# Where a pair's edge scores stand in the second layer of a two-layer graph network

## What is computed

```python
h = jnp.einsum('ni,hio->hno', x, W)                    # 4 heads of 64
attn_src = jnp.einsum('hno,hod->hn', h, a_src)
attn_dst = jnp.einsum('hno,hod->hn', h, a_dst)
e = attn_src[:, src_idx] + attn_dst[:, dst_idx]
e = jnp.where(e >= 0, e, NEG_SLOPE * e) * edge_weight[None, :]
e_exp = jnp.exp(e - jnp.max(e))
denom = jax.ops.segment_sum(e_exp.T, dst_idx, num_segments=num_nodes).T
alpha = e_exp / (denom[:, dst_idx] + 1e-10)
msg = h[:, src_idx] * alpha[..., None]                 # summed over dst, per head
```

## Time and profile before

| | us |
|---|---|
| median of 3 runs | 2435.32 |
| lowest, highest | 2430.52, 2443.21 |
| profiled execution | 2453.26 |
| its span | 2451.1 |
| mean granted TensorE clock | 0.886 |
| PE, DVE, POOL, ACT busy, share of the span | 79%, 62%, 60%, 56% |
| gathers of the second layer (L1351), 391 | 371.1 busy, 346.0 idle before |

### The profile page before, as it was taken

The page is one execution under the profiler, slowest core; times in us unless marked ns, Lnnn a source line. Parts: engine busy times, 40 slices in busy tenths (PEclk is TensorE's granted clock), DMA queues, the critical chain, the costliest instruction groups (busy, mean ns, idle before and its releaser), DMA issues. The chain is left out here.

```text
span 2451.1 us, 40398 instructions
## 1 busy us (share of the span) xinstructions
PE 1929.3 (79%) x12892; PEld 1704.4 (70%) x12892; DVE 1509.6 (62%) x3750; ACT 1382.8 (56%) x2780; POOL 1470.6 (60%) x1204
## 2 busy tenths in 40 slices
PE   7699999999999999999999999955134545544560
PEld 6588899988999999999999999954123333433440
DVE  6466666666666666666666666645155445444575
ACT  2488888888888888888888888845000000000012
POOL 0317778777777777767777777532645645654623
PEclk9899999999999999999999999977567667766785
DMA  5878877777777777777777777665434434444523
GB/s 198 287 204 182 196 165 169 170 166 166 160 160 158 159 159 159 157 161 154 158 159 158 158 158 159 131 158 138 107 87 120 129 106 123 129 110 109 134 83 108
DMA packets 236167, 370.81 MB, mean 151 GB/s; under 512 B 35853, under 2 KB 168935, under 8 KB 235949
## 3 DMA queue, kind: packets, MB, share of 16 engines
q0 software_dynamic: 101232, 188.20, 38.7%
q1 hardware_dynamic: 134717, 179.94, 24.4%
HBM read 270.57 MB, written 97.45 MB: 150 GB/s over the span
## 5 line engine op out<-in xcount | busy, mean ns | idle before, releaser
L1316 POOL DMA_INDIRECT accA<-ystage,to_a x391 | 650.2, 1663 | 231.0 <-issue 108.0
L1322 POOL DMA_INDIRECT GA<-TA,src_c x391 | 425.1, 1087 | 328.7 <-issue 93.3
L1351 POOL DMA_INDIRECT Hg<-HT,src_c x391 | 371.1, 949 | 346.0 <-DVE xb L913 168.7
L1861 ACT ACTIVATE drop<-neg_m 128x1 f32<-128x1 f32 x49 | 14.5, 295 | 627.3 <-DVE neg_m L908 517.1
L1420 PE MATMUL bank<-h1h,W1h 128*128 128x512 f32 x882 | 349.2, 396 | 1.3 <-DVE h1l L539 0.7
L1422 PE MATMUL bank<-h1h,W1l 128*128 128x512 f32 x882 | 348.0, 395 | 0.0
L1421 PE MATMUL bank<-h1l,W1h 128*128 128x512 f32 x882 | 347.0, 393 | 0.0
L539 DVE TENSOR_TENSOR h2l<-h2f,h2h 128x512 fp32r<-128x512 f32 (+1 forms) x294 | 202.8, 690 | 202.4 <-issue 87.3
L1628 PE MATMUL bank<-xb,in_window 128*128 128x260 f32 (+1 forms) x782 | 249.7, 475 | 70.3 <-issue 69.2
L539 DVE TENSOR_TENSOR h1l<-h1f,h1h 128x512 fp32r<-128x512 f32 x294 | 194.9, 690 | 131.2 <-ACT h1h L1698 112.9
L1628 PEld LDWEIGHTS bank<-xb,in_window 128*128 128x128 f32 (+1 forms) x782 | 182.4, 241 | 122.4 <-issue 87.3
(11 more groups left out here) (209 smaller groups left out, 5235.1 us busy)
## 6 DMA issues: line engine op xcount, KB each, us to landing
TW<-TB SPq DMA_DIRECT2D x196, 203.0 KB
ef<-in_eT SPq DMA_DIRECT2D x97, 256.0 KB
bcast_i<-in_src_row SPq DMA_DIRECT2D x97, 256.0 KB
HB<-hist SPq DMA_DIRECT2D x98, 130.0 KB
rel<-RL SPq DMA_DIRECT2D x97, 128.0 KB
rem<-RD SPq DMA_DIRECT2D x48, 256.0 KB
TB<-stB SPq DMA_DIRECT2D x24, 406.0 KB
accA<-zeros SPq DMA_DIRECT2D x4, 1677.0 KB, 13.0
```

The source lines that it names most:

```text
L1316: return pool.indirect_dma_start(out=table, out_offset=bass.IndirectOffsetOnAxis(ap=rows, axis=0), in_=sums, in_offset=None, compute_op=AL ...
L1322: pool.indirect_dma_start(out=GA[0:n, b % (GAR * BLOCKS_PER_GROUP), :].bitcast(f32), out_offset=None, in_=TA, in_offset=bass.IndirectOffse ...
L1351: pool.indirect_dma_start(out=Hg[0:n, slot, :], out_offset=None, in_=HT, in_offset=bass.IndirectOffsetOnAxis(ap=src_c[0:n, b:b + 1], axis= ...
```

## The change

On DVE `edge_scores(q+2)` moves from behind `carry_window(2q-1)` to between `running_maximum(q+1)` and `weighted_rows(2q+1)`, and `one_hot(q+3)` moves ahead of `window_rows(q+1)`. On PE `spread_maxima(q+2)` moves between the window sums of the pair's two groups. No function changes inside, no instruction, wait or buffer is added or taken away.

```diff
@@ vector
                 if 0 <= q + 1 < NQ:
                     running_maximum(q + 1)
+
+                if 0 <= q + 2 < NQ:
+                    edge_scores(q + 2)
                 if 0 <= q < NQ:
                     weighted_rows(2 * q + 1)
                 if 0 <= q - 1:
                     carry_window(2 * q - 1)
-                if 0 <= q + 2 < NQ:
-                    edge_scores(q + 2)
+                if q + 3 < NQ:
+                    one_hot(q + 3)
                 if 0 <= q + 1 < NQ:
                     window_rows(q + 1)
-                if q + 3 < NQ:
-                    one_hot(q + 3)
@@ tensor
             for q in range(-3, NQ):
                 if q >= 0:
                     window_sums(2 * q)
-                    window_sums(2 * q + 1)
                 if 0 <= q + 2 < NQ:
                     spread_maxima(q + 2)
+                if q >= 0:
+                    window_sums(2 * q + 1)
                 if q + 3 < NQ:
                     destination_scores(q + 3)
```

## The result

The changed kernel took 2419.47 us (median of 9 runs, 2414.77 to 2421.94) against 2432.28 (9 runs, 2429.91 to 2443.21): ratio 0.9944, 95% interval 0.9928 to 0.9960. The forecast of 2465 has the wrong sign; its range, 2400 to 2525, holds the time. The profiled execution of the changed kernel took 2417.07, its span 2414.9.

A forecast was written before the change was run, and what follows sets the result against it. No engine is full: waits between POOL's gathers and DVE's edge_scores set the pace. 42.9 pairs at 14.1 us plus 14 for window_scores give 619 against 592; with 3 at the end, +30 us: 2465 on the median, range 2400 to 2525.

The forecast's parts named there:

- Mechanism: Second layer's edge loop: bursts of 8 gathers, a pause of some 5 us after each, edge_scores waiting nearly every turn.
- the sum: Edge loop, one pair: 2.59 + 8.75 + 2.8 = 14.1 us against 13.5; with window_scores 619 against 592.
- the last term: Time from a burst's last gather's start to DVE's release at edge_scores: taken as 2.8 us, upper bound 4.15.
- the lower bound: Least time from the last gather's start to DVE's release at edge_scores: 2.74 us, from a burst of 7.
- The burst of seven: Seven gathers in the profile before, 2345.02 to 2352.52; DVE's release came 2.74 us after the last one's start.
- (b): On DVE, one_hot(q+3) ahead of window_rows(q+1): every set of scores now lies inside a burst, some 3.3 us in.
- the inner rival: Scores of q+3 come through inside the burst, 10.2 us after POOL's restart: 12.8 us a pair, 2406; 22%.
- (a): On DVE, edge_scores(q+2) moves ahead: 2.59 us instead of 4.11 from release to POOL's restart, 1.5 gained per burst.
- (c): On PE, spread(q+2) goes between the two groups' sums, ready ahead of POOL's restart; costed at zero.
- The POOL-bound rival: Something other than gathers delays edge_scores' s_ad and this order lifts it: POOL's 10.0 us a pair, 2272; 10%.

The follow-up runs named there:

- The hold made by hand: Either order plus an edge_scores wait for the last issuable gathers: new 2476.99 us, old 2560.45, old in every second pair 2416.45; kernel before 2258.05.
- DVE's order alone: Kernel before with only the DVE half of the change, TensorE in its old order: 2433.11 us on chip 1, ratio 1.0012.
- a third of the score products: Kernel before with 8 instead of 24 matmuls for a pair's destination scores: ratio 0.9837 on chip 0, where the kernel before takes 2433.57 us.

## Why the prediction was wrong

**Mechanism: right in the main.** The gathers come mostly in bursts of eight with one pause a pair (28 of 44 bursts); POOL waits 43 times for weighted rows, as written (about 43); edge_scores waits in 36 turns where 40 or more were forecast, 6.0 us in a burst of eight and 7.7 on average where 7 were; from edge_scores to the restart it is 2.58 where 2.59 was worked out; the scores stand 3.4 us into the burst where 3.3 was. The hold made by hand shows the sum itself to be sound, in both orders.

**The step that failed: the last term.** The prediction has "It grows with the burst, so I take 2.8, next to 7", with 2.74 as the lower bound. It measured 1.21 in the timeline and 1.25 on average over the bursts of eight. 2.59 + 8.75 + 1.25 = 12.6 a pair against 13.5, not 14.1. The 339 gathers behind the opening burst are 42.4 pairs: 534 us. window_scores costs some 1.8 us in each of six turns (2.3 forecast), 11 in all; that makes 545, where the profile has 552. The other 7 lie around `last_rows`, some small operations that DVE makes once (from 1810.5 on; 8.8 us in the old order). The kernel before has them too, within its 592, so the prediction's sum, which leaves them out, compared unlike things by that much. With the prediction's 42.9 pairs and without `last_rows` it would be 551, which agrees with 552 only because the two errors cancel.

The lower bound was the error behind it. It rested on "all issued gathers have to land first", an assumption that no row had shown; the release at 1.21 comes before the last gather has landed, at 2.8. The earlier trace rows had a release with gathers still being issued; I read it as an exception and gave it to a rival, instead of letting it open the bound to zero. And "that time no row shows for 8 gathers" wasn't so. The kernel before has this, timelines of POOL and DVE:

```profile
2277.55 0.94 POOL L1351 DMA_INDIRECT Hg<-HT,src_c  x1 [0.92 <-issue]
...
2286.31 0.95 POOL L1351 DMA_INDIRECT Hg<-HT,src_c  x1 [0.30 <-issue]
2286.98 0.19 DVE L875 TENSOR_TENSOR score<-Hg,bank 128x32 f32<-128x32 f32 x1 [7.02 <-remote]
```

These eight gathers follow eight others after 0.92 us of idle time, so they are no clean case; but the release comes 0.67 us behind the last of them, far under 2.74. With the bound at 0 the same sum would have run from about -90 to +87 us, with no change in the middle.

**What the term is made of.** Where a hold lasts in full, DVE goes on 11.35 us after the first gather in a burst of 8 (16 of 28 with DVE's order alone), 17.1 in one of 12 and 22.9 in one of 16: 1.44 us more for each gather, where POOL starts one every 1.25. That is why the last term grows with the burst, 2.6, 3.3 and 4.1. So 2.8 was close to the full hold at eight gathers. What the prediction missed is that the scores can come through about one such step sooner (10.0 instead of 11.35), as they do in 27 of 28 bursts of the first profile and 22 of 28 on chip 1.

**The burst of seven.** It gave the term by its length alone. There the scores stood behind two groups of sums, 5.5 us in; here one group and 3.4 us. The prediction had named this difference in (b) and in the inner rival's favour, but not carried it into the term. On chip 1 both values, 1.2 and 2.6, come at one length and within one kernel; the changed order only makes the short one more frequent. What picks between them isn't shown.

**(a), (c): right.** 1.5 us a burst measured as 4.11 - 2.58 = 1.53 with the same hold in both orders. The spread costs nothing where it now stands. But its move was costed at zero, and by the traces on chip 1 it goes with a shorter term (1.5 against 2.1 on average). Neither half gained anything measurable alone.

**The rivals.** The inner rival (a release 10.2 us after the restart, 12.8 a pair, 2406) is the nearest to what came: 10.0 us and 12.55 a pair. Its place, inside the burst, was wrong: with eight gathers this time lies 1.2 us behind the last one's start. It had 22%. The POOL-bound rival (2272) doesn't come by the order, but is the state of the program on four of six chips of the experiments, and there the change is worth nothing: 1.0002 and 1.0015.

**What stays open.** What holds TensorE's completions on some chips. The gathers' packets are alike there and elsewhere (a packet of 4160 bytes takes 161 ns in the median on both kinds), a gather is issued every 1.25 us on both, and the granted clock in the loop is 0.68 to 0.72 with the hold and 0.76 to 0.82 without, where TensorE is also busier; no run here made the hold come or go by itself. Whether it belongs to the chip or to the session is open as well. And of the span's 36 us the medians show 13, since the profiled execution of before (2453.3) was longer than any of its timed runs (up to 2443.2).

## What to carry to other kernels

When a sum's sign hangs on one term that no row shows, look for the assumption that keeps its lower bound up, and let a single row that contradicts it open the bound; then say "no change" as long as the bounds lie on both sides. A wait that can't be reached can be put into the program by hand (here a wait for the last group that may be issued), and this prices each order with known ends. Profile a kernel on a second chip before tuning an order around a wait whose releaser the profile can't name: here 173 us, and all the worth of the change, were there on some chips (or in some sessions) only, and taking away the held wait on one operation put it on the next.

## What the runs showed of the hardware

The same program takes 2257 to 2260 us on four chips and 2431 to 2443 on two (and on the first), with executions of one chip within 1.5%. On the slower ones, completions of TensorE that fall into a run of indirect gathers by POOL arrive late. What completes in the first 4 us or so still gets through (the spread at 2150.36, 4.1 us into a burst, in the rows above). What is sent then mostly comes 1.2 to 4.2 us after the last gather's start, now and then inside a long burst, and with a third of the score products mostly inside it: 6.4 us after the scores were sent in bursts of 8, 16 in bursts of 16, 48 in the first. The rows of the matrix products themselves show nothing of it: they stand at the time at which they were sent, and products behind the held ones are sent on meanwhile (in the profile after, sums at 2114.12 behind scores at 2113.43). Releases in bursts of 8 lie 10.0, 10.6 or 11.3 us from the first gather, in steps of 0.7 us, and the full hold grows by 1.44 us a gather from 8 to 16. DVE's own operations beside the same gathers keep their durations (xb 1.21 us on both kinds of chip).
